# Attention softmax: one vector operation over both halves of a step in place of two

## What is computed

```python
qkv = x.reshape(Bs * H * W, C) @ W_qkv + b_qkv
qkv = qkv.reshape(B_, N, 3, HEADS, HD).transpose(2, 0, 3, 1, 4)
q, k, v = (qkv[0], qkv[1], qkv[2])      # q and k are then rotated (rope)
attn = jnp.einsum('bhnd,bhmd->bhnm', q * SCALE, k)
attn = attn.reshape(Bs, nWm, HEADS, N, N) + mask[None, :, None, :, :]
attn = jax.nn.softmax(attn, axis=-1).reshape(B_, HEADS, N, N)
out = jnp.einsum('bhnm,bhmd->bhnd', attn, v)
```

## Time and profile before

| What | Value |
|---|---|
| Median of three runs | 2486.26 us |
| Profiled execution, its own time | 2484.12 us |
| Span of that execution, first to last instruction | 2482.3 us |
| Instructions | 75405 |
| Mean granted TensorE clock over the span | 0.931 of full |

### The profile page before, as it was taken

One profiled execution on the slowest core, in us unless ns is written; L12 is line 12 of the kernel. 1 busy time (PEld: TensorE's weight loads), 2 busy tenths in 40 slices (PEclk: granted clock), 3 DMA queues, 4 the chain that ended last, 5 costly groups with the idle time before them and its releaser, 6 DMA issues. The chain is left out here.

```text
span 2482.3 us, 75405 instructions
## 1 busy us (share of the span) xinstructions
PE 2034.6 (82%) x30446; PEld 1079.9 (44%) x30446; DVE 1684.5 (68%) x3438; ACT 1167.8 (47%) x2597; POOL 1079.6 (43%) x1227
## 2 busy tenths in 40 slices
PE   6588878887898899868994029999997499999996
PEld 5455545554555455535552003444442133333332
DVE  5588898889888988872223964666665456556553
ACT  6476666666666566632223414444442044433330
POOL 0277767776777777749502823222220131111100
PEclk8799999999999999979997559999999599999997
DMA  8300000000000000002224941444444323444444
GB/s 228 98 23 22 22 19 22 22 22 19 22 22 22 20 23 22 22 14 68 97 96 159 405 181 49 116 146 130 143 126 114 118 58 104 122 129 129 117 101 103
DMA packets 249921, 215.55 MB, mean 87 GB/s; under 512 B 132592, under 2 KB 237808, under 8 KB 247536
## 3 DMA queue, kind: packets, MB, share of 16 engines
q1 hardware_dynamic: 249584, 210.81, 28.6%
HBM read 78.29 MB, written 75.50 MB: 62 GB/s over the span
## 5 line engine op out<-in xcount | busy, mean ns | idle before, releaser
L1176 POOL TENSOR_SCALAR l_x<-l_x,l_scale,l_shift 128x384 f32<-128x384 f32 x192 | 155.6, 810 | 600.5 <-PE banks L1403 600.5
L418 POOL TENSOR_TENSOR at_prob<-at_prob,at_inv 128x512 f32<-128x512 f32 x288 | 294.1, 1042 | 116.7 <-DVE at_inv L558 111.5
L484 ACT ACTIVATE at_prob<-at_prob 128x512 f32<-128x512 f32 x288 | 181.9, 632 | 335.2 <-DVE at_prob L548 335.1
L1366 PE MATMUL banks<-l_a,l_taps 128*32 128x384 f32 x3456 | 310.9, 490 | 8.4 <-ACT l_r L1226 8.4
L1381 PE MATMUL banks<-l_above,l_taps 128*32 128x384 f32 x1728 | 307.4, 489 | 4.0 <-issue 1.8
L1381 PE MATMUL banks<-l_below,l_taps 128*32 128x384 f32 x1728 | 306.2, 489 | 0.0
L600 PE MATMUL banks<-at_xn,at_w 128*64 128x256 f32 x2336 | 287.5, 389 | 1.8 <-ACT at_xn L436 1.4
L1236 ACT ACTIVATE l_above<-l_below 96x384 f32<-96x384 f32 x144 | 75.5, 524 | 416.6 <-DVE l_below L1309 416.6
L1309 DVE SCALAR_TENSOR_TENSOR l_below<-banks,l_b,l_old 128x384 f32<-128x384 f32 x144 | 89.0, 618 | 218.7 <-PE banks L1381 188.7
L1295 DVE COPY l_old<-l_a 32x384 f32<-32x384 f32 x576 | 208.5, 362 | 26.1 <-ACT l_a L1213 14.9
L399 POOL TENSOR_TENSOR at_turn<-at_turn,at_tables 128x256 f32<-128x256 f32 x292 | 215.4, 759 | 1.7 <-ACT at_turn L455 1.7
(11 more groups left out here) (142 smaller groups left out, 3625.2 us busy)
## 6 DMA issues: line engine op xcount, KB each, us to landing
l_x<-x_mid SPq DMA_DIRECT2D x48, 768.0 KB, 4.4
l_rows<-l_r SPq DMA_DIRECT2D x768, 48.0 KB, 2.0
at_k_bd<-at_k SPq DMA_DIRECT2D x1168, 16.0 KB, 1.8
load_raw<-in_x SPq DMA_DIRECT2D x36, 512.0 KB, 5.0
y<-c_y SPq DMA_DIRECT2D x96, 192.0 KB
bn_y<-y SPq DMA_DIRECT2D x8, 2304.0 KB, 11.6
x_mid<-x_res SPq DMA_DIRECT2D x8, 2304.0 KB, 15.7
x_mid<-l_x SPq DMA_DIRECT2D x24, 768.0 KB, 3.7
```

Of the source, the lines that this page charges most:

```text
L418: nc.gpsimd.tensor_tensor(prob[i][p][:, :, :], prob[i][p][:, :, :], inv[i][p][:, :].unsqueeze(2).broadcast_to([P, HEADS, WIN]), ALU.mult). ...
L484: nc.scalar.activation(prob[j % 2][p][:, :, :], prob[j % 2][p][:, :, :], ACT.Exp).then_inc(s["exped"], 1)
L1366: last = nc.tensor.matmul(grid(acc(k)[block_rows(c), :]), e[:, dy + 1, dx, :], a[:, k % A_RING, rows_, dx:dx + SIDE], start=(dy, dx) == TA ...
```

## The change

The two halves' maximum, subtraction, sum and reciprocal become one operation each with 1024 (or 16) elements a partition, and in masked rows the minimum too. The exponents and the multiplication by the reciprocals stay one operation a half, on one common tile `prob[i]` with axes bank, half, head, key. The semaphores of the merged operations now count steps, and those who wait for them wait for both halves at once.

```diff
-        prob = [[sh.sb(ctx, f"at_prob{i}{p}", [P, HEADS, WIN]) for p in range(2)] for i in range(2)]
+        prob = [sh.sb(ctx, f"at_prob{i}", [P, 2, 2, HEADS // 2, WIN]) for i in range(2)]
-        top = [sh.sb(ctx, f"at_top{p}", [P, HEADS]) for p in range(2)]
-        total = [sh.sb(ctx, f"at_total{p}", [P, HEADS]) for p in range(2)]
-        inv = [[sh.sb(ctx, f"at_inv{i}{p}", [P, HEADS]) for p in range(2)] for i in range(2)]
+        top = sh.sb(ctx, "at_top", [P, 2, HEADS])
+        total = sh.sb(ctx, "at_total", [P, 2, HEADS])
+        inv = [sh.sb(ctx, f"at_inv{i}", [P, 2, 2, HEADS // 2]) for i in range(2)]
@@ GpSimd
                 for p in range(2):
-                    pool.wait_ge(s["inv"], 2 * n + p + 1)
+                    if p == 0:
+                        pool.wait_ge(s["inv"], n + 1)
                     nc.gpsimd.tensor_tensor(
-                        prob[i][p][:, :, :], prob[i][p][:, :, :],
-                        inv[i][p][:, :].unsqueeze(2).broadcast_to([P, HEADS, WIN]),
+                        prob[i][:, :, p], prob[i][:, :, p],
+                        inv[i][:, :, p].unsqueeze(3).broadcast_to([P, 2, HEADS // 2, WIN]),
                         ALU.mult).then_inc(s["normed"], 1)
@@ ScalarE
                 for p in range(2):
-                    act.wait_ge(s["shifted"], n * 2 + p + 3)
-                    nc.scalar.activation(prob[j % 2][p][:, :, :], prob[j % 2][p][:, :, :],
+                    if p == 0:
+                        act.wait_ge(s["shifted"], n + 2)
+                    nc.scalar.activation(prob[j % 2][:, :, p], prob[j % 2][:, :, p],
                                          ACT.Exp).then_inc(s["exped"], 1)
@@ VectorE
                 dve.wait_ge(s["scores"], n + 1)
-                for p in range(2):
-                    src = ps_s[:, :, QUAD * p:QUAD * (p + 1)].rearrange("p b (h m) -> p b h m", m=WIN)
-                    out = prob[i][p][:, :, :].rearrange("p (b h) m -> p b h m", b=2)
-                    split = [P, 2, HEADS // 2, WIN]
-                    dve.wait_ge(s["turned"], n * 2 + p + 1)
-                    if row.masked:
-                        table = tables[:, T_LIM:T_LIM + WIN].unsqueeze(1).unsqueeze(1).broadcast_to(split)
-                        nc.vector.tensor_tensor(out, src, table, ALU.min).then_inc(s["limited"], 1)
-                        src = out
-                        dve.wait_ge(s["limited"], row.b * (2 * ROW_STEPS) + 2 * j + p + 1)
-                    nc.vector.reduce_max(top[p][:, :].rearrange("p (b h) -> p b h", b=2), src, AX.X)\
-                        .then_inc(s["top"], 1)
-                    dve.wait_ge(s["top"], 2 * n + p + 1)
-                    nc.vector.tensor_tensor(
-                        out, src, top[p][:, :].rearrange("p (b h) -> p b h", b=2).unsqueeze(3).broadcast_to(split),
-                        ALU.subtract).then_inc(s["shifted"], 1)
+                src = ps_s.rearrange("p b (h m) -> p b h m", m=WIN)
+                out = prob[i][:, :, :, :, :].rearrange("p b w h m -> p b (w h) m")
+                both = [P, 2, HEADS, WIN]
+                dve.wait_ge(s["turned"], n * 2 + 2)
+                if row.masked:
+                    table = tables[:, T_LIM:T_LIM + WIN].unsqueeze(1).unsqueeze(1).broadcast_to(both)
+                    nc.vector.tensor_tensor(out, src, table, ALU.min).then_inc(s["limited"], 1)
+                    src = out
+                    dve.wait_ge(s["limited"], row.b * ROW_STEPS + j + 1)
+                nc.vector.reduce_max(top[:, :, :], src, AX.X).then_inc(s["top"], 1)
+                dve.wait_ge(s["top"], n + 1)
+                nc.vector.tensor_tensor(out, src, top[:, :, :].unsqueeze(3).broadcast_to(both),
+                                        ALU.subtract).then_inc(s["shifted"], 1)
                 turn_k(n + 2)
                 if j >= 2 and not row.first:
                     add_projection(row, j - 2)
-                for p in range(2):
-                    dve.wait_ge(s["exped"], 2 * n + p + 1)
-                    nc.vector.reduce_sum(total[p][:, :], prob[i][p][:, :, :], AX.X).then_inc(s["summed"], 1)
-                    dve.wait_ge(s["summed"], 2 * n + p + 1)
-                    nc.vector.reciprocal(inv[i][p][:, :], total[p][:, :]).then_inc(s["inv"], 1)
+                dve.wait_ge(s["exped"], 2 * n + 2)
+                nc.vector.reduce_sum(total[:, :, :], out, AX.X).then_inc(s["summed"], 1)
+                dve.wait_ge(s["summed"], n + 1)
+                nc.vector.reciprocal(inv[i][:, :, :, :].rearrange("p b w h -> p b (w h)"),
+                                     total[:, :, :]).then_inc(s["inv"], 1)
@@ TensorE
-                pe.wait_ge(s["shifted"], n * 2 + 2)
+                pe.wait_ge(s["shifted"], n + 1)
-                            prob[i][p][:, 2 * hp:2 * hp + 2, :].rearrange("p h m -> p (h m)"),
+                            prob[i][:, hp // 2, p, hp % 2 * 2:hp % 2 * 2 + 2, :].rearrange("p h m -> p (h m)"),
```

More of the change, by code:

```diff
@@ L517, in _ @@
             dve.sem_inc(s["added"], 1)
-            dve.sem_inc(s["shifted"], 2)
+            dve.sem_inc(s["shifted"], 1)
             def turn_k(q):
```

## The result

The changed kernel takes 2603.18 us (median of 4 runs, 2598.65 to 2604.64) against 2485.49 for the kernel before in the same session: the ratio is 1.047, 95% interval 1.0452 to 1.0489. It is slower by 118 us; 114 were forecast. The profiled execution took 2598.65 us, with a span of 2596.9.

The account below looks back on a forecast made before the run. A closed chain of 6.48 us a step without slack, not VectorE, bounds attention; 20 x 43.64 + 4 x 55.3 = 1094 us against 979.7, +114, gives 2598 (2600 against the median); range 2565 to 2635, or 2660 with lost time kept.

Parts of the forecast that it names:

- The chain: Unmasked attention step, score to next score through maximum, subtraction, exponents, value matmuls, projection: 6.48 us becomes 7.52, without projection 6.68.
- the second half: Skill's rule on grouping: if the engine isn't saturated but causes bubbles elsewhere, breaking instructions up may end sooner; time rises.
- VectorE's own loop: Maximum to next maximum, through second exponents, merged sum and reciprocal: 6.78 us, deciding over 6.68 in steps without projection.
- GpSimd's release: GpSimd waits once for both reciprocals; loop through k's transfers 19.8 us over three steps, 6.6 a step, under 7.27: covered.
- Masked rows: 4 of 24 block rows, minimum merged too: steps of 9.47 us with projection, 8.73 without, row 55.3 us.
- surcharge x: Extra time of the merged masked subtraction, reading SBUF twice beside GpSimd's work: 0 to 0.9 us, taken as 0.7.
- the clock: Rival: TensorE's clock falls to 1.2 GHz in masked rows as its busy share drops: up to 64 us, 2664; 3%.
- the forecast's list of signs of being wrong: Score to score under 6.5 us, merged operation near 0.9 or 1.4, scores mostly awaiting transfers, or attention's granted clock under 1.00.
- Lost time: Rival: 52 us lost in attention to late transfers or VectorE's backlog stay on top instead of being covered: 2652; 18%.
- VectorE as the bound: Rival: VectorE bounds attention, so merging's saving of 0.69 us a step shortens it by 99 us: 2387; 7%.
- The exponents' wait: ScalarE's total wait for VectorE's subtraction, ahead of the exponents: up from 335 to about 480 us.
- The sum and its range: Whole kernel: +114 us, to 2598 or 2600; 2565 to 2635, from masked subtraction (17 down, 5 up) and merged operations (17).

Follow-up runs that it names:

- the first experiment: Changed kernel with minimum, maximum and subtraction one half at a time again, sum and reciprocal still merged: 2528.3 us, ratio 1.0207 to the kernel before.

## Why the prediction was right

**The chain, 6.48 + 1.04 = 7.52 us.** Right, and the largest term. Measured 7.55 or 7.56, with the merged operations at 1206 and 1225 ns against 1.21 us from the slope of the earlier trace rows:

```profile
L554 DVE TENSOR_REDUCE at_total<-at_prob 128x16 f32<-128x1024 f32 x143 | 174.4, 1220 | 73.6 <-ACT at_prob L486 73.4
L548 DVE TENSOR_TENSOR at_prob<-banks,at_top 128x1024 f32<-128x1024 f32 x120 | 147.0, 1225 | 4.1
L546 DVE TENSOR_REDUCE at_top<-banks 128x16 f32<-128x1024 f32 x120 | 144.7, 1206 | 50.7 <-PE banks L627 50.7
```

Of the Trainium skill's rule (Perfetto Trace Analysis, Optimizing Scalar/DVE Operations), the second half held: with the engine at 63% and others waiting for it, the grouped operations finished later.

**VectorE's own loop, 6.78 us without projection.** Right in kind: 6.82 at the first step of a row (6.71 at the last), and it vanishes when the sums are split. An unmasked row was to be 43.64 and is 43.87, because the second step of a row takes 7.67 and not 7.52. With the sums split a row is 43.65, by steps of other lengths.

**GpSimd's release, covered.** The number came out right, the account had a hole. I followed the loop over three steps through the transfers of k (6.6 us a step) and never closed the one that leaves it at `turn_k` and returns through VectorE's order: 7.30 us. In the changed kernel 7.55 covers it by 0.25, so the forecast was not hurt; the forecast of the first experiment was, by over 20 us.

**Masked rows, 55.3 us.** Near by two errors that cancel: measured 55.0 to 57.2. The surcharge x on the subtraction was taken as 0.7, so that it was to last 1.9 us; its median is 1478 ns, so x is 0.25:

```profile
L548 DVE TENSOR_TENSOR at_prob<-at_prob,at_top x24: 1224/1478/1546, 327.4 to 1204.5; 128x1024 f32<-128x1024 f32 x24
```

I had let both engines run slower side by side. The timeline shows instead that one waits for the other:

```profile
352.97 1.42 POOL L399 TENSOR_TENSOR at_turn<-at_turn,at_tables 128x256 f32<-128x256 f32 x2
...
353.98 1.49 DVE L548 TENSOR_TENSOR at_prob<-at_prob,at_top 128x1024 f32<-128x1024 f32 x1
354.47 1.59 POOL L405 TENSOR_TENSOR at_q<-at_turn 128x256 f32<-128x256 f32 x1
```

The subtraction starts 0.41 us before L399 ends and lasts 1.49 us, where it takes 1.22 at the least. L405 takes 0.73 by itself; here its record is 1.59 long, and it ends 0.59 behind the subtraction. The Trainium skill (SBUF — State Buffer, SBUF: two separate sides) calls their shared port pair an exclusive lock rather than a split of bandwidth. These rows agree, and the surcharge, 0.27 us here, stays under the 0.41 us that was left of GpSimd's operation; that this bounds it in general is argued from them. The other error was the clock: given 3% as a rival that would hold everywhere, it came in single stretches instead, up to four in a masked row and just behind it, and costs 12 to 15 us. A granted clock under 1.00 in this stage was also on the forecast's list of signs of being wrong: of this sign it was wrong, while the time stayed near. Without the clock's part a masked row is 53.3 us.

**Lost time, 52 us, covered or kept (18%).** It was covered: unmasked rows but the first (40.7) and those behind a masked row (44.5 or 44.6) are 43.8 to 44.3 us. What those 52 us had been is clearer now. Before, the loops of 6.48 and 6.71 and VectorE's own work of some 6.2 us lay close together, and in the late steps VectorE, held by the loop of 6.71, fell behind the chain: that is the 0.13 to 0.19 us in the steps of 6.62 and 6.67. Up to 2 us are lost at the start of a row. With the second loop shortened these starts lost less, but they lose time even with both loops shortened, so the backlog is not all of it and the rest stays open.

**VectorE as the bound (7%).** It falls: 53.5 us less work, 118 us more time. The saving was also mis-sized, at 99 us: I added durations that overlap by 0.08 or 0.09 us at a boundary, the reciprocal of 16 takes 253 ns, not 203, and the merged sum 1220 ns, not some 1150.

**The exponents' wait**, forecast near 480 us, is 456.

**The sum and its range.** That +114 met 114.6 in the span is in part luck. The stage grew by 120.2 us: the unmasked rows took 877 us where 873 were forecast and the masked ones some 4 more than their 221, and the rest of the profiled execution was 5.6 us shorter. The change doesn't touch that rest, which is 8 us longer in the repeated run of the changed kernel, so it wanders by as much from execution to execution. The range has a slip: its terms, 5 and 17 us upwards, end at 2622, not 2635. The 2603 us lie within either.

## What to carry to other kernels

Merging two operations saves the merged engine a fixed cost and makes its consumer wait for the second half: here 0.5 us each for two of them, in a chain that had no slack. Before merging, find every loop that closes over a step, also those that close only because of the order on an in-order engine, and write each one's length down; the longest decides, and one that lies 0.25 us under it decides as soon as the first is cut. Where an operation in such an order needs nothing that comes late and is itself needed late (the copies of v, the added projection), moving it was worth 46 us, without a single instruction less.

## What was not expected of the hardware

- TensorE's granted clock fell from 1.00 to 0.50 for stretches of 3.4 us in masked steps in which TensorE was at work 6.3 of 9.06 us and, ahead of the first fall, stood idle at most 2.4 us in one piece. Five small matmuls a step kept it at 1.00. In the kernel before, the masked row, with steps of 8.13 us, is at 1.00. The Trainium skill (Perfetto Trace Analysis, Matmul Optimizations) says that the engine scales its power with use; the granted clock of these rows, 1.00 with the five added matmuls and 0.50 at times without them, agrees.
- VectorE's and GpSimd's operations on two SBUF inputs took turns: 1.49 and 1.59 us where they take 1.22 and 0.73 alone.
